# Attention scores spread over the slots in threes, fours and fives, two of them ahead of slot 0

## The reference

```
def _L0_xattn_ref(query, key, value, Wq, bq, Wk, bk, Wv, bv, Wo, bo):
    Q = proj(query, Wq, bq)            # (x @ W.T + b), split into 16 heads
    K = proj(key, Wk, bk)
    V = proj(value, Wv, bv)
    scores = jnp.einsum('bhqd,bhkd->bhqk', Q, K) / SCALE
    attn = jax.nn.softmax(scores, axis=-1)
    out = jnp.einsum('bhqk,bhkd->bhqd', attn, V)
    return out.transpose(0, 2, 1, 3).reshape(B, S, D) @ Wo.T + bo

x = x + jnp.tanh(g_xattn[0]) * _L0_xattn_ref(_layernorm(x), ctx, ctx, ...)   # x, ctx: (8, 512, 512)
x = x + jnp.tanh(g_ffn[0]) * _L0_ffn_ref(_layernorm(x), ...)                 # 8 experts, top 2
```

## Time and profile before

| what | value |
|---|---|
| median of three runs | 1789.11 us |
| profiled execution | 1788.94 us, its span 1787.2 us |
| TensorE busy | 1698.6 us, 95% of the span |
| VectorE, ScalarE, GpSimd busy | 1056.1, 799.5, 540.7 us |
| row maxima (line 969) | 512, 327.7 us busy, 686 ns each |
| scores for the maxima (line 1390) | 512, 171.8 us busy |
| one batch of the loop | 105.05 us, from the output product at 439.93 us to the next at 544.96 us |

### The profile page before, as it was taken

The page is one execution under the profiler, slowest core; times in us unless marked ns, Lnnn a source line. Parts: engine busy times, 40 slices in busy tenths (PEclk is TensorE's granted clock), DMA queues, the critical chain, the costliest instruction groups (busy, mean ns, idle before and its releaser), DMA issues.

```text
span 1787.2 us, 29087 instructions
## 1 busy us (share of the span) xinstructions
PE 1698.6 (95%) x10115; PEld 826.5 (46%) x10115; DVE 1056.1 (59%) x2083; ACT 799.5 (45%) x1093; POOL 540.7 (30%) x524
## 2 busy tenths in 40 slices
PE   7999999999999999999719999999999999999997
PEld 4324243332424334242206556474655647465563
DVE  6768867687786868767686525254352625434331
ACT  4563736446373654636314425162442516244240
POOL 2353635435363543626201211211111121111101
PEclk9999999999999999999859999999999999999999
DMA  6334263443425343432203634536263452626312
GB/s 222 115 66 147 73 174 109 115 137 83 150 80 161 122 108 124 97 98 94 110 33 113 175 78 134 145 100 165 52 178 71 142 137 100 162 63 177 70 38 29
DMA packets 214606, 203.17 MB, mean 114 GB/s; under 512 B 121812, under 2 KB 162912, under 8 KB 210456
## 3 DMA queue, kind: packets, MB, share of 16 engines
q1 hardware_dynamic: 193432, 181.80, 33.7%
q0 software_dynamic: 21120, 20.67, 6.7%
HBM read 134.57 MB, written 43.63 MB: 100 GB/s over the span
## 4 chain that ended last, share of the span: by engine, by line
PE 77%; DVE 13%; issue 4%; POOL 2%; DMA 1%; ACT 1%; SPq 1%; DVEq 0%; POOLq 0%; ACTq 0%
PE psum L1643 23%; PE psum L1619 21%; PE psum L1380 6%; PE psum L1409 5%; PE psum L1390 5%; PE psum L1507 5%; DVE mx L969 5%; PE psum L1424 4%; PE psum L1400 4%; PE psum L1435 2%; POOL pt L628 1%; DVE reached L1132 1%; DVE x2hl L1052 1%; DVE x2hl L1054 1%; SPq L489 1%
## 5 line engine op out<-in xcount | busy, mean ns | idle before, releaser
L1643 PE MATMUL psum<-w,hT 128*128 128x512 f16 (+1 forms) x1920 | 415.7, 379 | 0.0
L1619 PE MATMUL psum<-xgT,w 128*128 128x308 f16 (+1 forms) x3072 | 408.1, 293 | 0.5 <-DVE xgT L1233 0.5
L969 DVE TENSOR_REDUCE mx<-psum 128x1 f32<-128x512 f32 x512 | 327.7, 686 | 90.8 <-PE psum L1390 88.4
L1619 PEld LDWEIGHTS psum<-xgT,w 128*128 128x128 f16 x3072 | 296.1, 97 | 109.4 <-DVE xgT L1233 0.9
L1643 PEld LDWEIGHTS psum<-w,hT 128*128 128x128 f16 (+1 forms) x1920 | 199.3, 104 | 213.8
L895 ACT ACTIVATE h<-psum,b1c 128x308 f32<-128x308 f32 (+1 forms) x256 | 118.0, 512 | 340.8 <-PE psum L1619 340.3
L704 POOL DMA_INDIRECT out_dram<-y,idx_now x40 | 87.3, 2184 | 499.0 <-DVE y L1286 312.4
L1254 DVE TENSOR_TENSOR hT<-h,hT 128x615 f16<-128x615 f32 x128 | 102.5, 801 | 210.2 <-ACT hT L898 210.2
L1283 DVE SCALAR_TENSOR_TENSOR y<-psum,b2b 128x512 f32<-128x512 f32 (+1 forms) x40 | 27.7, 692 | 270.2 <-PE psum L1643 270.2
L1390 PE MATMUL psum<-stk 96*128 96x512 f16 x512 | 171.8, 383 | 10.5 <-DVE mx L969 1.5
L1380 PE MATMUL psum<-actT,wT 128*128 128x512 f16 x768 | 179.2, 381 | 2.0 <-DVE wT L956 2.0
(11 more groups left out here) (218 smaller groups left out, 1805.9 us busy)
## 6 DMA issues: line engine op xcount, KB each, us to landing
stage<-in_L_ffn_W_dram SPq DMA_DIRECT2D x62, 1024.0 KB, 5.3
stk<-qk_rows SPq DMA_DIRECT2D x192, 128.0 KB, 2.6
qk_rows<-qks SPq DMA_DIRECT2D x64, 256.0 KB, 2.6
xin<-in_x_dram SPq DMA_DIRECT2D x8, 1024.0 KB, 5.4
cin<-in_ctx_dram SPq DMA_DIRECT2D x8, 1024.0 KB, 7.5
xres<-in_x_dram SPq DMA_DIRECT2D x8, 1024.0 KB, 5.6
out_dram<-xres SPq DMA_DIRECT2D x32, 256.0 KB, 2.2
x_split<-x2hl SPq DMA_DIRECT2D x32, 256.0 KB, 2.3
```

The lines of the kernel that those rows point to most:

```text
L969: v.reduce_max(mx[:, KT * t + qt:KT * t + qt + 1], ps, AX.X).then_inc(read, 1)
L1619: mm = t_.matmul(psum[:, (2 * m + ch) % 4, 0:c1 - c0], w1[:, wp, kt, m * P:(m + 1) * P], xgT[:, KT * xp + kt, c0:c1], start=(kt == 0 and ( ...
L1643: mm = t_.matmul(psum[0:rows, Y_BANK[i], :], hT[:, hp, k, c * P:c * P + rows], w2[:, wp, k, :], start=(k == 0 and (hp, wp) == (0, 0)), sto ...
```

## The change

Scores are numbered j = 0 to 63, four to a head, and no longer belong to the slot of their head. Two are computed between the two value tiles ahead of slot 0. Slots 0 to 7 compute four each. From slot 8 on, slots without a ones product compute three and those with one five. `PLACES` says where in a slot they stand: 3 is two at the start, none in the middle, one at the end; 5 is two, two, one. The wait for the stacked heads stands before the first score of each group of four heads. The maxima rows stay in slots 4, 8, 12 and 16. The high halves of the next inputs go to slots 7, 10, 12, 14 and 16, and GpSimd's inverse deviations for tiles 2 and 3 go one step ahead, before the split of k 0.

```diff
--- before.py
+++ after.py
@@ -44,6 +44,11 @@
 LAG_B, LAG_C = 6, 7
 SLOTS = UNITS + LAG_C
 LN_SLOT = 1
+SCORES_FIRST = 2
+SCORES = (4, 4, 4, 4, 4, 4, 4, 4, 3, 3, 5, 3, 5, 3, 5, 3)
+SCORES_UP_TO = [SCORES_FIRST + sum(SCORES[:s]) for s in range(UNITS + 1)]
+PLACES = {3: (2, 2, 3), 4: (2, 3, 4), 5: (2, 4, 5)}
+NEXT_HI = {7: ((1, 0),), 10: ((1, 1), (1, 2)), 12: ((1, 3), (0, 0)), 14: ((0, 1), (0, 2)), 16: ((0, 3),)}
 QK_FIRST, QK_SLOT = 4, (0, 1, 3, 4)
 V_FIRST, V_SLOT = 2, (5, 6)
 X2T_SLOT, PARTS_SLOT, LG_SLOT = 2, 4, 5
@@ -57,6 +62,7 @@
 SUM_COUNT = len(SUM_ORDER)
 GROUP_SUMS = [[i for i, (kind, n) in enumerate(SUM_ORDER) if n // (2 if kind == "pair" else 4) == g] for g in range(NG)]
 SUMS_END = [max(slot for slot in SUMS for term in SUMS[slot] if SUM_ORDER.index(term) in GROUP_SUMS[g]) for g in range(NG)]
+MAXIMA_TURNED = [next(s for s in range(UNITS + 1) if SCORES_UP_TO[s] >= 16 * g + 16) for g in range(NG)]
 GROUP_NORM = [16, 18, 20, 23]
 GROUP_SPLIT = [17, 19, 21, 23]
 X_NORM_SLOT = (5, 5, 6, 6)
@@ -77,12 +83,22 @@
     return SUM_ORDER.index(("pair", u // 2) if u < 2 * PAIRS else ("unit", u))
 
 
+def slot_scores(s, place):
+
+    if s >= UNITS:
+        return []
+    if s < 0:
+        return list(range(SCORES_FIRST))
+    ends = (0,) + PLACES[SCORES[s]]
+    return [SCORES_UP_TO[s] + i for i in range(ends[place], ends[place + 1])]
+
+
 def later_v(s):
 
     return [V_FIRST + j for j, slot in enumerate(V_SLOT) if slot == s]
 
 
-C_HI_SLOT, C_LO_SLOT, X_HI_SLOT, X_LO_SLOT = 7, 17, 11, 16
+C_LO_SLOT, X_LO_SLOT = 17, 16
 
 
 class Banks:
@@ -260,10 +276,11 @@
                 banks.add(("qk", i), (2, 4, 0, 1)[i])
             for tt in range(V_FIRST):
                 banks.add(("v", tt), (3, 5)[tt])
+            for j in slot_scores(-1, 0):
+                banks.add(("S", j), j % 2)
             for s in range(SLOTS):
-                for qt in range(2):
-                    if s < UNITS:
-                        banks.add(("S", s, qt), qt)
+                for j in slot_scores(s, 0):
+                    banks.add(("S", j), j % 2)
                 for i in later_qk(s):
                     banks.add(("qk", i), (2, 4, 2, 4)[i - QK_FIRST])
                 if s == X2T_SLOT:
@@ -275,9 +292,8 @@
                     banks.add(("v", tt), (3, 6)[tt - V_FIRST])
                 if s == LG_SLOT:
                     banks.add("lg", 7)
-                for qt in range(2, KT):
-                    if s < UNITS:
-                        banks.add(("S", s, qt), qt - 2)
+                for j in slot_scores(s, 1) + slot_scores(s, 2):
+                    banks.add(("S", j), j % 2)
                 if 0 <= s - LAG_B < UNITS:
                     for hf in range(2):
                         banks.add(("ST", s - LAG_B, hf), (2, 4)[hf])
@@ -601,8 +617,8 @@
                 heads_stacked(pool, b)
                 for i, (which, m) in enumerate(QK_ORDER):
 
-                    if i in (0, 2) and not first:
-                        for tt in (i, i + 1):
+                    if i in (0, 1) and not first:
+                        for tt in (2 * i, 2 * i + 1):
                             inverse_deviation(1, tt, KT * b + (tt - KT))
                     n = "qk".index(which)
                     if i == QK_FIRST + 2:
@@ -817,9 +833,9 @@
                     if t >= LAG_B:
                         for tt in later_v(t):
                             values(tt)
-                    for n, slot in ((1, C_HI_SLOT), (0, X_HI_SLOT)):
-                        if not last and slot <= t < slot + KT:
-                            next_hi(n, t - slot)
+                    if not last:
+                        for n, tt in NEXT_HI.get(t, ()):
+                            next_hi(n, tt)
                     if t in GROUP_END[:-1]:
 
                         gr = GROUP_END.index(t)
@@ -962,11 +978,10 @@
             v.memset(stk[96:98, 1, :, :], SQ * SQ).then_inc(k_ones, 1)
 
             def batch(b, last):
-                def maxima(t, qts):
-                    if t < UNITS:
-                        for qt in qts:
-                            ps, read = filled(dve, use, ("S", t, qt), b)
-                            v.reduce_max(mx[:, KT * t + qt:KT * t + qt + 1], ps, AX.X).then_inc(read, 1)
+                def maxima(js):
+                    for j in js:
+                        ps, read = filled(dve, use, ("S", j), b)
+                        v.reduce_max(mx[:, j:j + 1], ps, AX.X).then_inc(read, 1)
 
                 def inverse_sums(g):
                     if g < NG - 1:
@@ -993,12 +1008,13 @@
                     v.scalar_tensor_tensor(hl[:, D:2 * D], src, (1.0, SX)[n], hl[:, 0:D],
                                            ALU.mult, ALU.subtract).then_inc(lo_ready[n], 1)
 
+                maxima(slot_scores(-1, 0))
                 for t in range(SLOTS + 1):
-                    maxima(t, (0, 1))
-                    if t % 4 == 0 and 4 <= t <= UNITS:
-                        g = t // 4 - 1
-                        for qt in (2, 3):
-                            copied(dve, use, ("S", 4 * g + 3, qt), b)
+                    maxima(slot_scores(t, 0))
+                    if t in MAXIMA_TURNED:
+                        g = MAXIMA_TURNED.index(t)
+                        for j in (16 * g + 14, 16 * g + 15):
+                            copied(dve, use, ("S", j), b)
                         best = mx[:, 16 * g:16 * g + 16]
                         v.tensor_scalar(mhl[:, g, 0:16], best, -1.0 / SQ ** 2, None, ALU.mult).then_inc(max_hi, 1)
                         dve.wait_ge(max_hi, NG * b + g + 1)
@@ -1008,7 +1024,7 @@
 
                         dve.wait_ge(mrow_in[g], 64 * b)
                         v.transpose(mrow[:, g, :], mhl[:, g, :]).then_inc(mrow_ready, 1)
-                    maxima(t, (2, 3))
+                    maxima(slot_scores(t, 1) + slot_scores(t, 2))
                     for n, slot in ((1, C_LO_SLOT), (0, X_LO_SLOT)):
                         if not last and slot <= t < slot + KT:
                             next_lo(n, t - slot)
@@ -1383,11 +1399,14 @@
                     if 1 in halves:
                         last.then_inc(bank_full[bank], 1)
 
-                def scores(s, qt):
-
-                    if s < UNITS:
-                        dst, full = claim(pe, use, ("S", s, qt), b)
-                        t_.matmul(dst, stk[0:96, 0, s, qt * P:(qt + 1) * P], stk[0:96, 1, s, :],
+                def scores(s, place):
+
+                    for j in slot_scores(s, place):
+                        h, qt = j // KT, j % KT
+                        if j % 16 == 0:
+                            pe.wait_ge(stk_in[j // 16], 96 * b + 96)
+                        dst, full = claim(pe, use, ("S", j), b)
+                        t_.matmul(dst, stk[0:96, 0, h, qt * P:(qt + 1) * P], stk[0:96, 1, h, :],
                                   start=True, stop=True).then_inc(full, 1)
 
                 def less_maxima(u, hf):
@@ -1453,16 +1472,14 @@
 
                 for i in range(QK_FIRST):
                     queries_keys(i)
-                for tt in range(V_FIRST):
-                    values(tt)
+                values(0)
                 if first:
                     pe.wait_ge(k_ones, 1)
+                scores(-1, 0)
+                values(1)
                 for s in range(SLOTS):
 
-                    if s % 4 == 0 and s < UNITS:
-                        pe.wait_ge(stk_in[s // 4], 96 * b + 96)
                     scores(s, 0)
-                    scores(s, 1)
                     filling(s, 0)
                     u = s - LAG_B
                     if u == 0:
@@ -1474,9 +1491,9 @@
                     less_maxima(u, 0)
                     if s < UNITS:
                         with_ones(s)
-                        scores(s, 2)
+                        scores(s, 1)
                     less_maxima(u, 1)
-                    scores(s, 3)
+                    scores(s, 2)
                     if 0 <= s - LAG_C < UNITS:
                         v_ = s - LAG_C
                         if v_ < KT:
```

## The result

The kernel after takes 1816.05 us (median; 1815.15 to 1818.3) against 1789.01 before: a ratio of 1.0155 [1.0142, 1.0167], 27 us slower. That is 1 us outside the predicted range. The profiled execution took 1815.15 us with a span of 1813.4; before it was 1788.94 and 1787.2. Its mean granted clock is 0.978.

What follows compares the result with a forecast made beforehand. TensorE was taken to bound the kernel: 1788.9 + 16.95 (first batch 2.35, six loop batches 11.7, last 2.9) + 1.7 for one clock drop = 1807.6, put down as 1807.5 us; range 1798 to 1815.

Steps and rivals of the forecast that it cites:

- Two scores ahead of slot 0: Batch start on TensorE: waiting for the heads, slot 0 starts 2.37 us later in loop batches, 2.45 first, 3.01 last.
- The landing: When the stacked heads' transfers arrive at batch start: 465.12 in the loop, 3.41 us after the last three began issuing.
- Deviations: GpSimd's inverse deviations one step sooner: VectorE is ready earlier, saving the 0.30 us wait in slot 0, six loop batches only.
- Slots 8 to 15: Slots of three and five scores: short ones gain, long ones lose, slots 8 and 9 wait; -0.1 us a batch.
- Rival B: Rival, 15%: start costs as forecast, but slots 8 to 15 or 2 and 3 gain 1 us a batch more; 1798 to 1800.
- D: Rival, 6%: the heads' wait of 1.9 us is cancelled by Rival B's gain at its largest; 1789 us.
- High halves: ScalarE copies moved to long slots and slot 16: cost nothing, or 0.2 us twice a batch if cover is gone.
- The clock: After TensorE's new waits: one drop to 1.2 GHz, for the longest wait, 1.7 us; possible none to eight, 0 to 13.6.
- rival A: Rival, 20%: the clock falls in half or more of the batches, four to eight drops; 1812.7 to 1819.5 us.

Runs made afterwards that it cites:

- The two runs: Kernel after without early scores (three- and five-score slots, deviations sooner): high halves moved, 1788.83 us; high halves in slots 7 to 14 as before, 1786.73 us.
- the fill: Kernel after with eight extra products, their result overwritten, put into TensorE's wait ahead of the two early scores: 1809.31 us, ratio 1.0112.
- the shorter wait: Kernel after with the two early scores in the middle of the second value tile: 1797.72 us, ratio 1.0052.
- the longer: Kernel after with the two early scores ahead of both value tiles: 1846.38 us, ratio 1.0325.

## Why the prediction was wrong, step by step

**Two scores ahead of slot 0: right, and a little too small.** In batch 4 slot 0 begins 28.44 us after the output product in place of 25.91, 2.53 later; predicted 2.37. The landing was put at the last batch's latency; in this batch it is 0.15 later. The table's 18.1 us for start and slots stand against a sum of 16.95. By batch: the first was put at 2.35 and is 1.99 longer, because the heads came at 45.22 and not at 45.74; the loop batches were put at 1.95 and are 2.2 longer, 0.15 by the landing and 0.1 by slots 8 to 15; the last was put at 2.9 and is 3.0 longer without the clock. So errors of both signs stand in the 1.15. The wait follows the place of the scores: in the loop nothing behind both tiles, 0.55 to 0.77 us in mid-tile, 1.83 to 1.93 behind one tile and 4.33 to 4.53 ahead of both.

**Deviations: right alone, and of no effect inside the change.** Alone they give 0.30 us a loop batch. In the kernel after slots 0 to 8 take 30.30 us, 30.60 before, which is the 0.30 of the sum. But with the two scores ahead alone, where the deviations stand as before, the same slots take 30.29. Where TensorE starts later, VectorE is ready without this part, so the number came out and its reason did not.

**Slots 8 to 15: right.** 27.75 us against 27.77, predicted 0.1 less. Short slots take 2.61 us, long ones 4.46. The first ones product kept its 7.49 us from slot 8, so the 1.08 of slots 8 and 9 turned into waits: 0.82 for GpSimd and 0.17 for a row of maxima, where I had put more than 1 us on GpSimd alone. The consequence was not drawn: the two scores done ahead were taken from slots where time saved turns into a wait, while slot 15 gave 0.85 us a batch for the same two. With the additions held, versions with and without the threes and fives agree within 0.6 us. Without the hold the version with them is slower by its median, 0.4 us with the high halves as before and 2.5 with them moved, though the loop batches of the traces are equal. Rival B's hidden waits did not come, and D with them.

**High halves: at nothing, not contradicted.** The two runs differ by 2.1 us in their medians and by nothing in the loop batches of their traces.

**The clock: the step that failed.** I took one drop, 1.7 us, because the 1.99 us gap of the earlier trace rows stood among transposes and the new ones in dense products. The profile shows the worth of four: one behind each of two waits of 1.87 and 1.92 us and two for the 3.93 of the last batch, 6.8 us. That is rival A by its sum (1812.7 to 1819.5, given 20%), though only three of the eight batches had a drop; the range ended at 1815 and so held only the lowest part of A. What the waits do to the clock is shown by the fill (no drop at that place in any batch), by the shorter wait (no drop) and by the longer (one in each batch). Against the argument from dense products stand the drops behind 1.87 and 1.92 us: they came in dense products too.

The row of 1.99 us was no firm ground either. The same wait before the same 48 products stands in every profiled execution (1.99 us, once 2.08), here in that of the deviations alone:

```profile
28.82 10.52 PE L1380 MATMUL psum<-actT,wT 128*128 128x512 f16 x48 [1.99 <-DVE wT L956]
```

The products take 10.52 us instead of the 12.21 of the earlier trace rows: no drop. In nine of the fourteen profiled executions the clock fell there and in five it did not. So a gap of this length is to be priced with a share of a drop each time, and for eight of them that is more than one drop. It also means that two executions can differ by 1.7 us near their start, where the kernels are the same.

**Not foreseen: the late row**, 1.4 us. The contention behind it was to be seen before: in its loop batches the pair of small operations for the last row takes 2.03 us, 0.38 elsewhere, and the row is already 0.28 us late for TensorE. So any further delay is paid in full. In one batch of after the first operation took 3.29. That GpSimd's additions are the cause is shown by holding them back: the pair drops to 0.38 and the wait is gone.

The miss of the profiled execution adds up: 5.1 for the clock, 1.15 for start and slots, 1.4 for the late row, 7.65 in all, is 1815.15 - 1807.5.

**Open.** Why a wait of 1.9 us drops the clock in some batches and not in others, and why a small operation gets through between two additions in most batches and not in a few. How many low stages the other executions of after had (1815.43 to 1818.3) is known only roughly: their mean granted clocks are 0.976 and 0.977 against 0.978, and a stage of 3.4 us at half clock lowers the mean of such a run by 0.001, so by this estimate they had one or two more. The kernel after with additions held was not run, so the late row's share in those is argued from its relatives.

## What to carry to other kernels

On an in-order engine, work put ahead of a tile makes the tile wait for that work's operands. Look up the landing first. If it is after the new place, price the idle time, and add half of a low-clock stage for each gap of a length behind which the trace of that kernel has shown one, times the share of such gaps that had one, not for the longest gap alone. If every slot's distance to a fixed release stays the same, moving work between slots moves nothing: when work is taken out of a slot, take it where no such release follows. A tiny operation on the path of a row can take many times its time beside a streaming one on another engine (0.63 to 3.29 us instead of 0.17). Holding the other engine back for its length gained 2 us here, where the whole schedule change lost 27.

## What was not expected of the hardware

- Idle time of 1.87 and 1.92 us on TensorE, at the start of a batch, was followed by 3.4 us at 1.2 GHz in two of six loop batches of after, while 1.83 to 1.93 us in the others was not. The 1.99 to 2.08 us near 29 us was in nine of fourteen profiled executions. 0.55 to 1.12 us in the attention never was; 2.31 us once was not; 2.92 us once was. 3.28 to 5.4 us always was, by 6.8 us at 1.2 GHz in all cases but one (4.33 us, followed by 3.4). In the filled kernel 1.75 us in another place was.
- A VectorE operation on 128x16 elements took 0.17 us, and 0.63 to 3.29 us beside GpSimd's additions of 128x512 f32, which take 1.3 us each. At its longest it ended only with the last of four additions in a row. Held apart, the pair took 0.38 us.
- Six loads issued together (3.02 us of issuing) had all landed only 0.3 us sooner than the last three of two separate groups, though those three were issued 0.6 us sooner.
